# A whole prologue ahead of the first round of scores, in an attention and expert kernel on one Trainium2 core

## The chip, the cores and the metric

The kernel runs on one core of one Trainium2 chip. The metric is the device time of one execution in microseconds (us). Five engines take part, each with its own list of instructions: PE (TensorE, the matmuls), ACT (ScalarE), DVE (VectorE), POOL (GpSimd) and SP (SyncE, which here only issues DMAs). They meet through semaphores: an instruction adds to one when it is done, and another engine waits until it has reached a value.

## The reference, cut to what matters

2048 tokens of 128 features go through an attention layer with 16 heads of 8 features, then through a layer of eight experts of which each token takes two, plus one expert shared by all. The change touches the attention alone:

```python
q = _l2norm(split_heads(x_norm @ Wq))
k = _l2norm(split_heads(x_norm @ Wk))
v = split_heads(x @ Wv)
align = jnp.einsum('bhtd,bhsd->bhts', q, k)
resonance = jax.nn.sigmoid((align - THRESH) * SHARP)
gate_q = jnp.einsum('bhtd,d->bht', q, gq)
gate_k = jnp.einsum('bhsd,d->bhs', k, gk)
modulation = resonance * gate_q[..., :, None] * gate_k[..., None, :]
collapse = jnp.einsum('bhts,bhsd->bhtd', modulation, v)
```

Every query meets every key, so there are 16 x 2048 x 2048 sigmoids.

## The kernel before, in words

**Blocks and rounds.** The queries are cut into four blocks (`NB`) of 512 tokens (`TB`). For each block there are 64 rounds (`ROUNDS`): four sets of four heads, and for each set 16 slices of 128 keys. One round is: PE multiplies the keys of the slice with the queries of four heads (`scores`, L847, matmuls at L862) into two pairs of PSUM banks, ACT takes a sigmoid over each pair (`sigmoids`, L743, the instruction at L746, 128 x 1024 numbers each) and writes them into one half of `res`, and PE multiplies them with the values (`values`, L866, at L876), which add up in the bank `AV` over 16 rounds. PE issues the scores of a round ahead of the value products of the round before. After each 16 rounds DVE multiplies `AV` with the gate of the queries (`collapse`, L1250). In blocks 1 to 3, and in a last stretch without rounds, the work of the experts is laid between the rounds; block 0 has only the preparation of the expert weights on DVE beside it, from round 17 on.

**The prologue.** Before rounds can run, queries and keys have to be made, for four groups of 512 tokens, in six steps on several engines. *tokens*: DVE norms the tokens (L1179), PE transposes them (`turn_hidden`, L800, at L807) and ACT copies them out (L685). *project*: PE multiplies with the weights in four parts (`project_qkv`, L810, L822 to L824), and ACT evicts each (L694); PE goes two parts ahead at most. *square*: ACT squares (L698), DVE sums the squares (L1209), takes an inverse root in some ten small steps and scales the heads (`unit`, L1204, L1215), and makes the gated values (L1221). *high*: ACT makes the high half of queries and keys (L703), DVE the low half (`low_parts`, L1226, L1230), and POOL repeats both (L611, four instructions a group). *turn*: PE transposes queries and keys in four parts (`turn_qk`, L826, L842), and they are copied out, by ACT (`turn`, L706, L713) or, for the last group, by DVE (L1248); each copy adds one to `qk_copied`. Ahead of these last copies DVE makes the weights of the gate (`gate_weights`, L1190, L1192 to L1202).

**Banks.** The prologue uses the banks `GB`, `UB` and `OB`; `UB` and `OB` together are `UO`. A step waits where another still reads its bank: the transposes of the tokens of group 2, for instance, wait for all copies of the turn of group 0, and those of group 3 for the turn of group 1. The rounds use the four banks of `S` as two pairs, and `UO` as a third pair once the prologue has done with it.

**The order.** The list `PROLOGUE` (L89 to L92) sets the order in which PE and ACT issue the steps. ("rounds", n) in it stands for the next n rounds of block 0, on both engines; rounds 0 to 7 stand there, after which the loop over rounds goes on from round 8. DVE and POOL have orders of their own (L1239 to L1248 and L606 to L612), in which rounds do not occur. `WIDE_FROM` (L94) is the round from which the third pair is used: `score_pair` (L97) gives the pair of a half round, `scores_before` (L102) the number of sigmoids after which that pair is free, and in round `WIDE_FROM` PE waits at L859 for all sixteen copies:

```python
if (i, k, j) == (0, WIDE_FROM, 0):

    pe.wait_ge(qk_copied, 4 * NB)
```

Of the kernel before, what the change touches and what calls it, by code (L numbers as in the profile page):

```python
# [86 lines left out]


PROLOGUE = [("tokens", 0), ("project", 0), ("square", 0), ("tokens", 1), ("project", 1), ("high", 0),  # L89
            ("square", 1), ("turn", 0), ("tokens", 2), ("rounds", 1), ("high", 1), ("project", 2),  # L90
            ("square", 2), ("turn", 1), ("tokens", 3), ("rounds", 1), ("high", 2), ("project", 3), ("rounds", 1),
            ("square", 3), ("turn", 2), ("rounds", 2), ("high", 3), ("rounds", 3), ("turn", 3)]  # L92

WIDE_FROM = 9  # L94


def score_pair(n):  # L97

    return (n - 2 * WIDE_FROM) % 3 if n >= 2 * WIDE_FROM else n % 2


def scores_before(n):  # L102

    return max([m + 1 for m in range(max(n - 40, 0), n) if score_pair(m) == score_pair(n)], default=0)
# [16 lines left out]
def build(nc, x, wqkv, vecs, consts, ident16, wo, router, gu, down, out):  # L121
    ctx = ExitStack()
    with ctx:
# [330 lines left out]
        def wait(eng, s, value):  # L454

            if not isinstance(value, int) or value > 0:
                eng.wait_ge(s, value)
# [337 lines left out]
        def _(pe):  # L795
# [51 lines left out]
            def scores(i, k):  # L847
# [5 lines left out]
                for j in range(G):  # L853
                    if j % 2 == 0:

                        wait(pe, sig_done, scores_before(2 * (i * ROUNDS + k) + j // 2))
                        if (i, k, j) == (0, WIDE_FROM, 0):

# [793 lines left out]
```

## Time and profile before

| what | value |
|---|---|
| median of three runs | 727.62 us (724.76 to 728.91) |
| the profiled execution | 728.29 us |
| its span, first to last instruction | 726.5 us |
| mean granted TensorE clock | 0.94 |
| PE busy | 617.6 us (85%) |
| ACT busy | 565.6 us (78%) |
| DVE busy | 419.7 us (58%) |
| POOL busy | 163.4 us (22%) |
| chain that ended last | PE 70%, DVE 13%, issue 5%, ACT 3%, DMA 3%, POOL 2% |
| costliest line of that chain | PE AV L876, 36% |
| sigmoids of `S` and of `UO`, L746 | 348 of mean 1063 ns and 164 of mean 1065 ns |

The profile is of one execution. Times in it count from the start of the span. A row of the timeline gives the start, the time that is covered, the engine, the line of the kernel, the operation, the tile written and the tiles read, and how many instructions were merged; brackets hold the idle time of the engine ahead of it and what ended it. The granted clock is the share of the full 2.4 GHz that TensorE was given; 0.50 is the lower level of 1.2 GHz.

### The profile page before, as it was taken

The page shows a single profiled execution, that of the slowest core. Times are in us where ns is not written, and L with a number is a line of the kernel's source. Part 1 is how long each engine was busy: PE and PEld are TensorE (multiplying, and loading weights), DVE is VectorE, ACT ScalarE, POOL GpSimd, SP SyncE. Part 2 cuts the span into 40 slices and gives each one's busy share as a digit, 9 for nine tenths or more (in the row PEclk, how much of TensorE's full clock was granted, in tenths as well). Part 3 has the DMA queues.
Part 4 walks back from the last instruction along what each step waited for, and adds up shares of the span by engine and source line. Part 5 has one row for each costly group of instructions (what it writes and reads, how often), then busy time and mean ns, then how long its engine had stood idle before and what let it go on. Part 6 is the DMA issues. An engine that isn't in the chain of part 4 may idle for free.

```text
span 726.5 us, 15317 instructions
## 1 busy us (share of the span) xinstructions
PE 617.6 (85%) x5928; PEld 259.6 (36%) x5928; DVE 419.7 (58%) x1105; ACT 565.6 (78%) x663; POOL 163.4 (22%) x149
## 2 busy tenths in 40 slices
PE   3577999999999999999999999989999993475840
PEld 2453211112222344432334444323344441465840
DVE  6775184930552545538635865475458546665975
ACT  1578799999999999989899999888989991033510
POOL 1122000000032122200525212024441210245732
PEclk9999999999999999999999999999999997577975
DMA  8600001630034344410534445105434440293721
GB/s 325 230 30 30 30 9 19 259 111 1 9 107 139 112 132 145 136 51 2 176 116 143 146 130 141 33 22 173 138 113 136 142 131 1 71 333 135 229 79 51
DMA packets 47639, 82.02 MB, mean 113 GB/s; under 512 B 5456, under 2 KB 25168, under 8 KB 47568
## 3 DMA queue, kind: packets, MB, share of 16 engines
q1 hardware_dynamic: 45088, 76.31, 32.8%
q0 software_dynamic: 2048, 4.20, 2.1%
q8 instruction: 47, 0.77, 0.4%
q10 hardware_dynamic: 432, 0.54, 0.3%
q14 instruction: 24, 0.20, 0.1%
HBM read 64.59 MB, written 16.45 MB: 112 GB/s over the span
## 4 chain that ended last, share of the span: by engine, by line
PE 70%; DVE 13%; issue 5%; ACT 3%; DMA 3%; POOL 2%; SPq 1%; POOLq 0%; DVEq 0%
PE AV L876 36%; PE GB L950 14%; PE S L862 7%; PE UO L862 3%; PE GB L897 2%; ACT res L746 1%; DVE work L1381 1%; DVE gate_q L1540 1%; DVE coll L1257 1%; DVE work L1374 1%; PE GB L945 1%; POOL xs_dram L624 1%; DMA gu_ring<-gu_dram 1%; PE UO L842 1%; DVE work L1516 1%
## 5 line engine op out<-in xcount | busy, mean ns | idle before, releaser
L746 ACT ACTIVATE res<-S 128x1024 f32<-128x1024 f32 x348 | 348.8, 1063 | 22.8 <-PE S L862 11.2
L876 PE MATMUL AV<-res,vg 128*8 128x512 f32 x2048 | 305.2, 599 | 1.9 <-DVE coll L1257 1.8
L746 ACT ACTIVATE res<-UO 128x1024 f32<-128x1024 f32 x164 | 174.7, 1065 | 8.5 <-PE S L862 7.2
L650 POOL TENSOR_TENSOR work<-work 128x512 f32<-128x512 f32 x64 | 82.5, 1289 | 290.7 <-DVE work L1381 286.6
L862 PE MATMUL S<-qT,kT 32*128 32x512 f16 x696 | 104.3, 388 | 2.3 <-ACT res L746 2.1
L950 PE MATMUL GB<-xT,gu_ring 128*128 128x128 f16 x1128 | 81.7, 224 | 12.9 <-DVE place L1356 6.0
L721 ACT ACTIVATE work<-work,scl 128x512 f32<-128x512 f32 x64 | 46.7, 730 | 43.5 <-DVE work L1374 43.5
L1374 DVE TENSOR_SCALAR work<-GB,scl 128x512 f32<-128x512 f32 x56 | 45.3, 810 | 59.9 <-PE GB L950 59.3
L862 PEld LDWEIGHTS S<-qT,kT 32*128 32x128 f16 x696 | 25.7, 91 | 145.7 <-ACT res L746 93.5
L950 PEld LDWEIGHTS GB<-xT,gu_ring 128*128 128x128 f16 x1128 | 65.4, 100 | 34.0 <-issue 17.6
L624 POOL DMA_INDIRECT xs_dram<-xrow,slot x32 | 31.7, 990 | 185.4 <-DVE slot L1361 177.1
L862 PE MATMUL UO<-qT,kT 32*128 32x512 f16 x328 | 63.6, 384 | 0.0
L876 PEld LDWEIGHTS AV<-res,vg 128*8 128x8 f32 x2048 | 36.6, 87 | 72.1 <-ACT res L746 29.4
L1393 DVE TENSOR_TENSOR hid_lo<-work,hid_hi 128x512 f16<-128x512 f32 x64 | 49.2, 768 | 5.9 <-ACT hid_hi L736 4.4
L1381 DVE SCALAR_TENSOR_TENSOR work<-work,scl,GB 128x512 f32<-128x512 f32 x48 | 35.8, 746 | 27.6 <-PE GB L950 26.8
L1540 DVE TENSOR_SCALAR gate_q<-GB 128x512 f32<-128x512 f32 x16 | 11.0, 690 | 51.9 <-PE GB L887 51.9
L862 PEld LDWEIGHTS UO<-qT,kT 32*128 32x128 f16 x328 | 15.4, 90 | 67.3 <-ACT res L746 45.7
L950 PE MATMUL GB<-dn_ring,hid_hi 128*128 128x128 f16 x336 | 34.1, 224 | 6.0 <-DVE work L1374 2.6
L1401 DVE COPY xT<-GB 128x256 f16<-128x256 f16 x45 | 12.8, 291 | 38.1 <-PE GB L945 37.9
L1257 DVE TENSOR_TENSOR coll<-AV,gate_q 128x512 f32<-128x512 f32 x16 | 11.0, 689 | 36.1 <-PE AV L876 36.1
L950 PE MATMUL GB<-dn_ring,hid_lo 128*128 128x128 f16 x168 | 31.4, 224 | 0.0
L950 PEld LDWEIGHTS GB<-dn_ring,hid_hi 128*128 128x128 f16 x336 | 24.8, 100 | 16.5 <-issue 7.7
(252 smaller groups left out, 681.0 us busy)
## 6 DMA issues: line engine op xcount, KB each, us to landing
gu_ring<-gu_dram SPq DMA_DIRECT2D x54, 512.0 KB, 3.5
dn_ring<-dn_dram SPq DMA_DIRECT2D x56, 256.0 KB, 2.9
work<-in_gu SPq DMA_DIRECT2D x8, 512.0 KB, 10.5
gu_dram<-gu_ring SPq DMA_DIRECT2D x8, 512.0 KB, 2.7
ys_dram<-work SPq DMA_DIRECT2D x60, 64.0 KB, 2.7
work<-in_down SPq DMA_DIRECT2D x8, 256.0 KB, 10.9
dn_dram<-dn_ring SPq DMA_DIRECT2D x8, 256.0 KB, 2.9
kT<-gu_dram SPq DMA_DIRECT2D x4, 512.0 KB, 7.4
```

Source lines behind the costliest of these rows:

```text
L624: nc.gpsimd.indirect_dma_start(xs_dram, bass.IndirectOffsetOnAxis(ap=slot[:, i % 2, n:n + 1], axis=0), xrow[:, n % SUB, :], None).then_inc ...
L650: nc.gpsimd.tensor_tensor(hid[u % 2], prod[u % 2], sg[u % 2], ALU.mult).then_inc(hid_ready, 1)
L721: nc.scalar.activation(sg[c % 2], gate_c[c % 2], ACT.Sigmoid, scale=scale(S_SIG)).then_inc(sg_ready, 1)
L746: nc.scalar.activation(res[:, k % 2, 2 * half:2 * half + 2, :].rearrange("p h t -> p (h t)"), score_banks(i, k, half).rearrange("p h t -> ...
L862: mm = nc.tensor.matmul(banks[:, j % 2, :], kT[r, g, s * P:(s + 1) * P], qT[r, g, :], start=True, stop=True)
L876: mm = nc.tensor.matmul(AV[32 * j:32 * j + HD, :], vg[:, s, G * g + j, :], res[:, k % 2, j, :], start=s == 0, stop=s == ST - 1)
L950: mm = nc.tensor.matmul(bank, w, v, start=first and n == 0, stop=last and n == 2)
L1257: v.tensor_tensor(coll[:, g, :], AV[:], gate_q[:], ALU.mult).then_inc(coll_ready, 1)
L1374: v.tensor_scalar(gate_c[u % 2], gate_bank(i, u), scale(S_HI), scale(S_LO), ALU.min, ALU.max).then_inc(gate_clipped, 1)
L1381: v.scalar_tensor_tensor(out=prod[u % 2], in0=gate_c[u % 2], scalar=scale(S_PROD), in1=up_bank(i, u), op0=ALU.mult, op1=ALU.mult).then_inc ...
L1393: v.tensor_tensor(hid_lo[:, n % LAG], hid[u % 2], hid_hi[:, n % LAG], ALU.subtract).then_inc(hid_split, 1)
L1540: v.tensor_scalar(gate_q[:], GB[:], 1.0 / QK_SCALE, None, ALU.mult).then_inc(gateb_copied, 1)
```

## The change

The entries of the eight rounds are taken out of `PROLOGUE`, so that all steps of all four groups stand ahead of round 0, and `WIDE_FROM` becomes 0: the third bank pair is in use from round 0, and PE's wait for sixteen copies stands ahead of round 0 instead of round 9. What the rounds compute, and the order of the other steps, stays.

```diff
-            ("square", 1), ("turn", 0), ("tokens", 2), ("rounds", 1), ("high", 1), ("project", 2),
-            ("square", 2), ("turn", 1), ("tokens", 3), ("rounds", 1), ("high", 2), ("project", 3), ("rounds", 1),
-            ("square", 3), ("turn", 2), ("rounds", 2), ("high", 3), ("rounds", 3), ("turn", 3)]
-
-WIDE_FROM = 9
+            ("square", 1), ("turn", 0), ("tokens", 2), ("high", 1), ("project", 2),
+            ("square", 2), ("turn", 1), ("tokens", 3), ("high", 2), ("project", 3),
+            ("square", 3), ("turn", 2), ("high", 3), ("turn", 3)]
+
+WIDE_FROM = 0
```

## Rows read from the trace of the kernel before

**Rows 1.** Windows: length, busy time of each engine, granted clock, DMA share, GB/s.

```profile
82.50:92.50 10.00, 10.00 (x68) 1.64 (x64) 0.00 (x0) 10.00 (x13) 0.00 (x0) 1.00 0.01 2
...
36.30:79.20 42.90, 34.21 (x252) 17.58 (x252) 27.81 (x62) 32.86 (x44) 9.90 (x12) 0.88 0.08 32
```

**Rows 2.** The chain that ended last: start, duration, what; two pieces.

```profile
97.10 1.51 PE AV L876 x8
...
120.94 1.50 PE AV L876 x8
```

**Rows 3.** Timeline of ACT, prologue to round 10.

```profile
20.32 0.50 ACT L694 ACTIVATE pwork<-UO 128x400 f32<-128x400 f32 x1 [0.64 <-PE UO L824]
...
27.31 0.50 ACT L694 ACTIVATE coll<-UO 128x400 f32<-128x400 f32 x1 [0.64 <-PE UO L824]
...
43.59 0.50 ACT L694 ACTIVATE pwork<-UO 128x400 f32<-128x400 f32 x1 [0.64 <-PE UO L824]
...
49.97 0.60 ACT L685 ACTIVATE pwork<-UO 128x512 f32<-128x512 f32 x1 [1.13 <-PE UO L807]
...
64.20 3.93 ACT L746 ACTIVATE res<-S 128x1024 f32<-128x1024 f32 x4
68.03 1.15 ACT L703 ACTIVATE pwork<-coll 128x512 f16<-128x512 f32 x2
...
78.78 3.77 ACT L746 ACTIVATE res<-S 128x1024 f32<-128x1024 f32 x4 [4.05 <-PE S L862]
82.49 1.02 ACT L746 ACTIVATE res<-UO 128x1024 f32<-128x1024 f32 x1
```

**Rows 4.** Timeline of PE, prologue to round 8.

```profile
12.71 1.27 PE L822 MATMUL GB<-w_qkv,lnb_all 128*128 128x272 f32 x2 [0.69 <-ACT pwork L685]
...
22.45 0.72 PE L822 MATMUL GB<-w_qkv,lnb_all 128*128 128x272 f32 x2 [1.73 <-ACT pwork L685]
...
31.53 1.47 PE L842 MATMUL UO<-id,pwork 128*128 128x128 f16 x16 [4.25 <-POOL pwork L611]
33.35 1.92 PE L842 MATMUL UO<-id,pwork 128*128 128x128 f16 x16 [0.35 <-ACT qT L713]
...
37.75 0.73 PE L822 MATMUL GB<-w_qkv,lnb_all 128*128 128x272 f32 x2 [0.36 <-ACT pwork L685]
...
48.94 0.99 PE L807 MATMUL UO<-const_sb,tok 128*128 128x128 f32 x4 [1.18 <-issue]
...
52.23 0.83 PE L822 MATMUL GB<-w_qkv,lnb_all 128*128 128x272 f32 x2
...
63.72 1.90 PE L876 MATMUL AV<-res,vg 128*8 128x512 f32 x8
...
78.35 0.40 PE L862 MATMUL S<-qT,kT 32*128 32x512 f16 x4
```

**Rows 5.** Timeline of DVE, group 3 of the prologue.

```profile
60.50 1.22 DVE L1209 TENSOR_REDUCE ssq<-pwork 128x128 f32<-128x1024 f32 x1 [5.79 <-ACT pwork L698]
...
65.09 1.23 DVE L1215 TENSOR_TENSOR coll<-coll,rn_t 128x1024 f32<-128x1024 f32 x1
...
66.74 0.69 DVE L1221 TENSOR_TENSOR vg<-coll,gk_s 128x512 f32<-128x512 f32 x1
68.69 1.71 DVE L1230 TENSOR_TENSOR pwork<-coll,pwork 128x512 f16<-128x512 f32 x2 [1.25 <-ACT pwork L703]
...
72.69 0.28 DVE L1202 TENSOR_SCALAR gm_b<-const_sb,gq_parts 128x128 bf16<-128x128 f32 x1
76.37 1.29 DVE L1248 COPY y_tok<-UO 128x1024 f16<-128x1024 f16 x2 [3.40 <-PE UO L842]
77.86 1.29 DVE L1248 COPY kT<-UO 128x1024 f16<-128x1024 f16 x2 [0.19 <-PE UO L842]
```

**Rows 6.** Timeline of POOL, group 3 of the prologue.

```profile
68.74 3.30 POOL L611 TENSOR_SCALAR pwork<-pwork 128x512 f16<-128x512 f16 x4 [12.39 <-ACT pwork L703]
```

**Rows 7.** Window with PE's granted clock (1.00, third figure from the end).

```profile
36.40:38.00 1.60, 1.21 (x9) 0.77 (x10) 1.50 (x4) 0.90 (x2) 0.00 (x0) 1.00 0.05 10
```

## The prediction, made before the changed kernel had run

> **What bounds the kernel now.** I read the page first, for the share of the engines and the chain that ended last: it runs mostly through PE, above all through the value products of the rounds, and the slices of the span show that PE and ACT are not yet full in the prologue. Then come the stretches that the change touches. From 82.5 to 92.5 us both engines are busy all the time [rows 1]. The chain of waits shows what a round costs there: from the value products at 97.10 to those at 120.94 lie 13 rounds, so 23.84 / 13 = 1.83 us a round [rows 2]. ACT sets this: its two sigmoids of a round start some 0.91 us apart and follow each other without a gap. A round that isn't done early therefore costs 1.83 us later, and nothing hides it.
>
> In the prologue it is different. From 36.3 to 79.2 us ACT is busy 32.86 of 42.90 us and DVE 27.81 [rows 1]: neither is full, each waits for the other, for PE or for POOL. The sixteen sigmoids of rounds 0 to 7 stand by the list inside the prologue, the four of rounds 8 and 9 start at 78.78 us, and the first of round 10 starts at 82.49 us [rows 3]. From there on the changed kernel issues the same instructions in the same order with the same three bank pairs (the pair of a half round was already its number modulo 3). So the question is one number: **when does the first sigmoid of round 10 start?** Before: 82.49 us. Afterwards: end of the prologue, plus 0.43 us from the first scores at 78.35 to the first sigmoid at 78.78 [rows 3, 4], plus 10 x 1.83 = 18.33 us. The two are equal if the last copies of the prologue end at 82.49 - 18.33 - 0.43 = 63.7 us; they now end at 77.86 + 1.29 = 79.15 us [rows 5]. The prologue would have to become 15.4 us shorter.
>
> **The change part by part.** It takes eight rounds out of three instruction streams (ACT's sigmoids, PE's scores and value products). No DMA is added or removed. The only wait that moves is the one for all sixteen qk_copied copies: from round 9 to round 0, where PE's whole round loop stands behind it, and through it ACT's sigmoids. On SP the store of the last group's queries becomes due earlier with the copies; the next load into qT waits for round 15's scores anyway, and POOL's queue is passed by nothing. I follow the chain with everything at the full clock first.
>
> *Projection of group 2.* Up to its start at 37.75 us nothing changes [rows 4]. Undisturbed, a projection takes 4.86 us from its first matmul to the start of its last eviction (22.45 to 27.31 [rows 3, 4]), so 42.61 us instead of 43.59 [rows 3], where ACT had round 0's sigmoids ahead of the evictions: 0.98 us gained. The square, the turn of group 1 and the transposes of group 3 follow in the same order, so these start at 48.94 - 0.98 = 47.96 us.
>
> *Projection of group 3.* Before, PE did round 1's scores and value products between those transposes and the projection at 52.23 us [rows 4]. Without them it waits only for ACT's copy of their bank, which began 1.03 us after them and took 0.60 [rows 3], so until 49.59 us: start at 49.62, last eviction at 54.48, its square at about 55.0. The square had also stood behind round 2's sigmoids; DVE's reduction of it comes at 56.1 us instead of 60.50 [rows 5], 4.4 us gained.
>
> *DVE's chain of group 3.* From that reduction DVE works without a gap: heads scaled after 65.09 + 1.23 - 60.50 = 5.82 us, values after 66.74 + 0.69 - 60.50 = 6.93 us [rows 5]. This is work, not waiting, and keeps its length: 61.9 and 63.0 us. The high parts on ACT, which stood behind four sigmoids (64.20 to 68.03 [rows 3]), start at 61.95, so the low parts on DVE start at 63.0 instead of 68.69: 5.7 us gained. From the low parts to the end of the gate weights are 72.69 + 0.28 - 68.69 = 4.28 us: 67.3 us.
>
> *Turn of group 3.* POOL's repeats started 0.71 us after ACT's high parts and take 3.30 us [rows 3, 6]; the third of four is through at about 61.95 + 0.71 + 2.5 = 65.2 us, and PE's first transposes (16 in at most 1.92 us at half clock [rows 4]) by 67.1. Before, DVE waited 3.40 us here for a PE that was busy with rounds 5 to 7. That wait goes; **what is late next is DVE itself**, with the 2.65 us of gate weights that it does ahead of the copies and that the wait had covered. So the copies run from 67.3, and their 2.78 us (76.37 to 79.15 [rows 5]) end at 70.1 us: 9.1 us gained of the 15.4 needed. First sigmoid 70.57, round 10 at 88.90, against 82.49: **6.4 us lost**, at the full clock.
>
> *Clock.* Three places may run at half of it. Projection 3: the transposes of 48.94 ran at half clock (0.99 us [rows 4]) and PE stays as idle ahead of them. A projection that began cold took 7.61 us (12.71 to 20.32 [rows 3, 4]) against 4.86, so the price lies between 0 and 2.75 us. I take 1.4: before, the half clock covers the work from 48.94 until shortly after 52.23, where the first pair of matmuls took 0.83 us; if it ends at the same time again, 2.8 us of the projection that now begins at 49.62 run at half speed, and half of that is lost. Turn 3: sixteen cold transposes take 1.92 us [rows 4], at most half of which is the clock: 0 to 0.9, I take 0.4, since PE is nearly idle from 60 us on. First rounds: a cold set of value products takes 1.90 us [rows 4], with 0.4 of scores 0.47 more than a round; for three rounds 0 to 1.4. I take 0.4, because with three pairs PE starts a round ahead and round 0 has no products before it. That the third pair spares ACT its short gaps in rounds 0 to 8 is in the sum already, as each is priced at 1.83.
>
> On the clock two rules of the Trainium skill can be weighed. After 4.25 us of idling PE did two sets of sixteen transposes, the second in 1.92 us at half clock, and nothing else [rows 4]; from 36.4 to 38.0 us the granted clock is 1.00 [rows 7]. The page "TensorE: Matmul & The Clock Gate" of the Trainium skill says, in "Part 1: The HAM clock gate", that the throttled state is the default and that activity releases it; this speaks against the change, which takes scores and value products from between PE's pauses, and by that rule alone the clock terms would be at their upper ends, a loss of 11.5 us in all. The same page adds, in "Part 4: PE-mode transpose", that transpose mode does not count as busy in the same way; by that, turn 3 and the first rounds would be cold throughout, about 1.5 us more than my sum. The trace differs there: the clock rose on transposes alone.
>
> **Sum:** 6.4 + 1.4 + 0.4 + 0.4 = 8.6 us. The profiled execution took 728.29 us (span 726.5), 0.67 above the median of 727.62; from it the sum gives 736.9, and from the median, which is what a comparison sees, **736.2 us**.
>
> **Rivals.** *The waits fall further, and it is not slower.* Place: DVE's waits in the prologue. Price: all that DVE does not work from 36.3 to 79.2 is 42.90 - 27.81 = 15.1 us [rows 1]; were all of it to go, the copies would end at 64.1 and the kernel lose 0.4 us, 728.0. It decides from an end at 63.7 us. For it: every one of these waits is for ACT or PE, whom the change relieves. Against: DVE's reductions need squares of projections that need the bank which the preceding turn frees, and those steps stay. Halfway there, with half of the clock terms, it would lose 3.4 + 1.1 = 4.5: about 732.
>
> *PE cold throughout.* Both projections and all else at half clock: 6.4 + 2 x 2.75 + 0.9 + 1.4 = 14.2 us: 741.8. For it: fewer matmuls between the pauses, as the first clock rule above has it. Against: the clock was full from 36.4 on after transposes alone [rows 7].
>
> *The loss is absorbed later.* A slack in blocks 0 to 3 would take it up, about 727.6. Against: the stretch of [rows 2] is rounds and nothing else, and everything after round 10 is released by rounds, but for the first loads, which SP and ACT issue at the start and wait for nothing.
>
> That the change does something other than it says can be excluded from the code: half rounds 0, 1, 2 get the three pairs, and all users of the two borrowed banks are done when the wait is over.
>
> **How the numbers follow.** Forecast (6.4 to 11.5 us lost) 0.78; waits that fall further, about 4.5 lost, 0.08; down to no loss at all, 0.04; cold throughout 0.06; absorbed 0.04. The range takes in the forecast's bounds and half of the lighter case, less and plus the spread of the runs shown (724.76 to 728.91): 731.5 to 740.0. What such a measurement can tell from no change is about 0.5%, 3.6 us. Slower by more than that has the forecast, the cold case and part of the lighter one: 0.90; same 0.08; faster 0.02.
>
> **What the profile would show.** Right: no sigmoid before about 72 us; projection 3 starting near 49.6; DVE's last copies starting straight after the gate weights, ending at 70 to 73; the first sigmoid of round 10 near 91; after it the same intervals as before. Wrong: copies that end before 66 us, or after 75; a gap between DVE's gate weights and the copies; rounds 0 to 9 that take other than 18 to 19 us; a block 1 whose start is not shifted by the same amount.

## The result, and the profile of the changed kernel

The changed kernel took 741.48 us (median of four runs, 739.86 to 741.79) against 726.19 us before (the three runs of the table and a fourth of 724.05): a ratio of 1.0204, 95% interval 1.0162 to 1.0246, so about 15 us slower. A second set of five runs, taken later, gave 1.0176 (1.0155 to 1.0197), some 13 us. The direction was forecast, the size was not: 736.2 us had been said, and the range ended at 740.0.

The profiled execution has a span of 739.8 us, 13.3 more than before. ACT's timeline answers to [rows 3]; the row at 76.36 is the first sigmoids, and the last row, twenty half rounds on, is the first of round 10:

```profile
42.25 0.50 ACT L694 ACTIVATE pwork<-UO 128x400 f32<-128x400 f32 x1 [1.68 <-PE UO L824]
43.91 0.50 ACT L694 ACTIVATE pwork<-GB 128x400 f32<-128x400 f32 x1 [1.16 <-PE GB L824]
45.05 0.50 ACT L694 ACTIVATE pwork<-UO 128x400 f32<-128x400 f32 x1 [0.64 <-PE UO L824]
...
59.29 0.50 ACT L694 ACTIVATE coll<-UO 128x400 f32<-128x400 f32 x1 [0.64 <-PE UO L824]
...
66.76 1.15 ACT L703 ACTIVATE pwork<-coll 128x512 f16<-128x512 f32 x2 [2.23 <-DVE coll L1215]
76.36 1.94 ACT L746 ACTIVATE res<-S 128x1024 f32<-128x1024 f32 x2 [8.45 <-PE S L862]
...
80.82 1.02 ACT L746 ACTIVATE res<-S 128x1024 f32<-128x1024 f32 x1 [0.68 <-PE UO L862]
...
95.29 1.22 ACT L746 ACTIVATE res<-UO 128x1024 f32<-128x1024 f32 x1
```

Round 10 begins at 95.29 us instead of 82.49: 12.8 of the 13.3 us are lost by then, and the remaining half microsecond is spread over the rest. So the question of the prediction was the right one, and only its answer was off. The bracket of the first sigmoid shows where ACT's time went: it stands 8.45 us ahead of it with nothing to do. Before, its longest wait between 31 and 82 us was 4.05.

DVE's timeline, for [rows 5], and PE's, for [rows 4], show two different things:

```profile
60.92 1.22 DVE L1209 TENSOR_REDUCE ssq<-pwork 128x128 f32<-128x1024 f32 x1 [5.28 <-ACT pwork L698]
...
67.77 2.11 DVE L1230 TENSOR_TENSOR pwork<-coll,pwork 128x512 f16<-128x512 f32 x2
...
69.97 0.38 DVE L1194 TENSOR_TENSOR gq_parts<-vec_sb,gq 128x1 f32<-128x1 f32 x1
...
71.96 0.28 DVE L1202 TENSOR_SCALAR gm_b<-const_sb,gq_parts 128x128 bf16<-128x128 f32 x1
72.15 1.28 DVE L1248 COPY y_tok<-UO 128x1024 f16<-128x1024 f16 x2
74.03 0.69 DVE L1248 COPY kT<-UO 128x1024 f16<-128x1024 f16 x1 [0.59 <-PE UO L842]
74.88 0.69 DVE L1248 COPY kT<-UO 128x1024 f16<-128x1024 f16 x1 [0.16 <-PE UO L842]
```

```profile
30.29 1.86 PE L842 MATMUL UO<-id,pwork 128*128 128x128 f16 x16 [4.25 <-POOL pwork L611]
32.50 1.93 PE L842 MATMUL UO<-id,pwork 128*128 128x128 f16 x16 [0.35 <-ACT qT L713]
35.59 1.09 PE L807 MATMUL UO<-const_sb,tok 128*128 128x128 f32 x4 [1.16 <-issue]
37.36 1.27 PE L822 MATMUL GB<-w_qkv,lnb_all 128*128 128x272 f32 x2 [0.69 <-ACT pwork L685]
...
50.40 1.09 PE L807 MATMUL UO<-const_sb,tok 128*128 128x128 f32 x4 [1.17 <-issue]
52.17 1.27 PE L822 MATMUL GB<-w_qkv,lnb_all 128*128 128x272 f32 x2 [0.69 <-ACT pwork L685]
```

On DVE the forecast order holds: the copies follow the gate weights without a wait (72.15 right behind 71.96), where before there was one of 3.40 us. On PE the clock is the news. Both projections begin with a pair of matmuls of 1.27 us, the length that [rows 4] show for the cold one at 12.71; from the first matmul to the start of the last eviction they take 45.05 - 37.36 = 7.69 and 59.29 - 52.17 = 7.12 us, where the full clock needs 4.86. The window from 31 to 79 us, of the changed kernel and then of the one before, puts a number on it (the clock is the third figure from the end):

```profile
31.00:79.00 48.00, 30.88 (x193) 22.97 (x193) 32.00 (x73) 24.48 (x33) 10.25 (x12) 0.68 0.11 44
```

```profile
31.00:79.00 48.00, 37.41 (x280) 20.36 (x284) 32.66 (x75) 36.50 (x47) 10.86 (x14) 0.86 0.10 38
```

### The profile page after: what moved, and what is told of

It is laid out like the page before. It is cut to its first block, busy times and chain, and to the rows that moved or that the text cites. A ratio compares the mean times of both kernels' runs of the same rounds, so it can differ in the third digit from the quotient of the medians.

```text
span 739.8 us, 15318 instructions
## 1 busy us (share of the span) xinstructions
PE 624.5 (84%) x5928; PEld 264.8 (36%) x5928; DVE 419.7 (57%) x1105; ACT 565.9 (76%) x663; POOL 164.2 (22%) x149
## 4 chain that ended last, share of the span: by engine, by line
PE 73%; DVE 16%; issue 5%; POOL 2%; ACT 2%; DMA 2%; POOLq 0%; DVEq 0%; ACTq 0%
PE AV L876 36%; PE GB L950 15%; PE S L862 7%; PE UO L862 3%; PE GB L897 2%; DVE work L1374 2%; DVE work L1381 2%; DVE gate_q L1540 1%; DVE coll L1257 1%; PE GB L822 1%; PE GB L945 1%; POOL res L638 1%; DVE work L1516 1%; PE UO L950 1%; PE UO L842 1%
## 5 line engine op out<-in xcount | busy, mean ns | idle before, releaser
L746 ACT ACTIVATE res<-S 128x1024 f32<-128x1024 f32 x342 | 344.9, 1073 | 27.8 <-PE S L862 15.7
L746 ACT ACTIVATE res<-UO 128x1024 f32<-128x1024 f32 x170 | 182.4, 1073 | 8.5 <-PE S L862 7.2
L862 PE MATMUL S<-qT,kT 32*128 32x512 f16 x684 | 102.6, 388 | 1.6 <-DVE kT L1248 0.9
L862 PE MATMUL UO<-qT,kT 32*128 32x512 f16 x340 | 66.5, 388 | 0.0
L1401 DVE COPY xT<-GB 128x256 f16<-128x256 f16 x45 | 12.8, 291 | 38.2 <-PE GB L945 37.9
```

The lines of the kernel that those rows point to most:

```text
L746: nc.scalar.activation(res[:, k % 2, 2 * half:2 * half + 2, :].rearrange("p h t -> p (h t)"), score_banks(i, k, half).rearrange("p h t -> ...
L862: mm = nc.tensor.matmul(banks[:, j % 2, :], kT[r, g, s * P:(s + 1) * P], qT[r, g, :], start=True, stop=True)
```

## The experiments

Theory A: the rounds' sigmoids lose their cover, as forecast, and the clock falls further than priced. Rival B: the order of the steps costs all of it, and the half clock only goes along.

**Extra matmuls in PE's pauses.** `filler(n)` puts n matmuls of 272 columns into a score bank that round 0 overwrites; nobody reads them.

```diff
+            def filler(n):
+                for _ in range(n):
+                    nc.tensor.matmul(S[:, 0, 0:2 * D + H], lnb_all[:], w_qkv[:, 0:2 * D + H], start=True, stop=True)
...
+                        if b in (1, 2):
+                            filler(1)
                         pe.wait_ge(qk_copied, b * 4 + n - 1)
...
                     tokens += 1
+                    filler(1 if b > 1 else 0)
...
                     projected += 1
+                    filler(8 if b == 1 else 1 if b > 1 else 0)
...
                     turned += 1
+                    filler((2, 2, 14, 0)[b])
```

> The changed kernel, with extra matmuls of no use on PE wherever it pauses in the prologue (272 columns into a score bank that nobody reads before round 0 overwrites it), so that nothing but the granted clock should change. Theory A, the step that failed is the clock term: the granted clock is near 1.00 in the prologue, both late projections take about 4.9 us from first matmul to last eviction instead of 7.1 to 7.7, the first sigmoid of round 10 comes 6 to 8 us earlier than at 95.3 us, and the time is 733 to 736 us. Theory B, the half clock only goes along and the order of the steps costs the 15 us: about 741 us, or more where the extra matmuls get in the way.

Measured: 732.55 us (five runs, 731.38 to 733.7), ratio to the kernel before 1.0064 (1.0044 to 1.0083). By the ratios, useless work made the changed kernel 8 to 10 us faster. Its window, then rows of ACT and of PE:

```profile
31.00:79.00 48.00, 41.13 (x289) 25.87 (x288) 32.16 (x74) 30.61 (x40) 10.39 (x12) 0.96 0.11 45
```

```profile
41.49 0.50 ACT L694 ACTIVATE pwork<-UO 128x400 f32<-128x400 f32 x1 [0.64 <-PE UO L824]
...
53.13 0.50 ACT L694 ACTIVATE coll<-UO 128x400 f32<-128x400 f32 x1 [0.64 <-PE UO L824]
...
69.34 1.94 ACT L746 ACTIVATE res<-S 128x1024 f32<-128x1024 f32 x2 [7.59 <-PE S L869]
...
73.79 1.02 ACT L746 ACTIVATE res<-S 128x1024 f32<-128x1024 f32 x1 [0.68 <-PE UO L869]
...
88.26 1.22 ACT L746 ACTIVATE res<-UO 128x1024 f32<-128x1024 f32 x1
```

```profile
70.73 2.48 PE L883 MATMUL AV<-res,vg 128*8 128x512 f32 x8
73.14 0.61 PE L869 MATMUL S<-qT,kT 32*128 32x512 f16 x2
```

The granted clock is 0.96, the projections take 5.12 and 4.98 us, and round 10 begins at 88.26, against 95.29 without the extra matmuls: 7.0 us of the 12.8 go with the clock. About 0.5 of the 7.0 is won ahead of the transposes of group 2's tokens (35.06 us against 35.59), where none of the removed rounds had stood. One place stayed cold: the first value products and the scores behind them, where the granted clock is 0.50 from 72 to 74 us. The spans of the two profiles differ by 10.1 us; the 3.1 that lie behind round 10 can't be put down to the edit, because the same instructions stand there in every kernel of this document and took 641.4 to 646.2 us in the twelve profiles.

Theory B is out. What is left is near the part of the prediction worked out at the full clock, which had round 10 at 88.90.

**The third bank pair alone.** The changed kernel with its pairs as before:

```diff
-WIDE_FROM = 0
+WIDE_FROM = 9
```

> The changed kernel with the third bank pair from round 9 only, as before: the first part of the change alone. Theory A (three pairs from round 0 are worth little, but keep ACT fed while PE is cold): 0.5 to 2 us slower than the changed kernel, 742 to 743.5 us. Theory C (the early wait or the early third pair costs something): equal to the changed kernel or faster, 741.5 us or less.

Measured: 739.25 us, ratio 1.0158 (1.013 to 1.0186), so not slower than the changed kernel. My expectation fell. ACT's rows say why:

```profile
75.36 3.77 ACT L746 ACTIVATE res<-S 128x1024 f32<-128x1024 f32 x4 [6.94 <-PE S L862]
80.00 15.07 ACT L746 ACTIVATE res<-S 128x1024 f32<-128x1024 f32 x16 [0.86 <-PE S L862]
94.96 1.02 ACT L746 ACTIVATE res<-UO 128x1024 f32<-128x1024 f32 x1
```

Rounds 0 to 9 take 94.96 - 75.36 = 19.6 us on two pairs, 95.29 - 76.36 = 18.9 on three. But on two pairs round 0 needn't wait for DVE's last copies, which end here at 75.84: it starts 0.5 us ahead of them, while in the changed kernel it starts 0.8 us behind them (76.36 against 75.57). The third pair gains 0.7 us and its wait takes 1.3, and the runs show no gain from the two together. What lies in the order of the prologue is practically the whole loss.

**Three of the eight rounds.** The kernel before, with rounds 5 to 7 behind the last turn:

```diff
-            ("square", 3), ("turn", 2), ("rounds", 2), ("high", 3), ("rounds", 3), ("turn", 3)]
+            ("square", 3), ("turn", 2), ("rounds", 2), ("high", 3), ("turn", 3)]
-WIDE_FROM = 9
+WIDE_FROM = 6
```

> The kernel before with only rounds 5 to 7 moved behind the last turn, and the third pair from round 6. Theory A: three rounds put off cost 5.5 us, the wait of DVE for PE of 3.4 us goes; the first sigmoid of round 10 moves from 82.5 to about 85.4, with up to 1 us for a colder clock: 729 to 731 us. Theory B' (each of the eight rounds costs its eighth of the 15 us): 732 us. If the rounds were free in either place: 726 us.

Measured: 730.16 us (ten runs), ratio 1.0034 (1.0014 to 1.0054); round 10 begins at 86.12, 3.6 us later than before, as theory A had it with its 1 us for a colder clock (group 2's projection, whose instructions are those of before, took 1.1 us longer here). An equal share of the loss for each round, 3 / 8 of 15 us, would have been 5.6.

**Gate weights behind the copies.** In the changed kernel:

```diff
-            gate_weights()
-
             dve.wait_ge(q_saved, (NB - 1) * 16)
             for n in range(4):
                 dve.wait_ge(qk_tr, (NB - 1) * 4 + n + 1)
                 v.tensor_copy(*turned_bank(NB - 1, n)).then_inc(qk_copied, 1)
+            gate_weights()
```

> The changed kernel with DVE's gate weights (2.65 us) behind the last copies of the prologue instead of ahead of them. Theory A: they are on the path, but right behind them PE's cold transposes would be late next (first half done at about 71.4 us against copies that start at 72.15), so 0.7 us is gained, about 740.8 us. If DVE alone were late: 2.65 us, 738.8 us. If the gate weights were not on the path: 741.5 us.

Measured: 737.38 us, ratio 1.0123 (1.009 to 1.0156), more than expected. But round 0 gained 76.36 - 73.70 = 2.66 us in the profile, of which 66.76 - 64.90 = 1.86 are there already when ACT makes the high parts of group 3, ahead of anything that the edit touches. That leaves 0.8 us for it, as expected. The rest is a warmer group 2: its projection took 6.54 us here instead of 7.69. The transposes ahead of it ran at the full clock (0.63 us) and its first pair nearly so, but then it fell to half clock all the same:

```profile
37.70 0.95 PE L822 MATMUL GB<-w_qkv,lnb_all 128*128 128x272 f32 x2 [0.69 <-ACT pwork L685]
...
39.78 1.11 PE L822 MATMUL UO<-w_qkv,lnb_all 128*128 128x272 f32 x2
```

DVE's rows, here with a wait of 1.74 us for PE's cold transposes, confirm what is late next:

```profile
69.75 1.48 DVE L1246 COPY y_tok<-UO 128x1024 f16<-128x1024 f16 x2 [1.74 <-PE UO L842]
71.64 1.49 DVE L1246 COPY kT<-UO 128x1024 f16<-128x1024 f16 x2 [0.41 <-PE UO L842]
...
73.22 0.16 DVE L1194 TENSOR_TENSOR gq_parts<-vec_sb,gq 128x1 f32<-128x1 f32 x1
```

**The same two again**, to see what was chance.

> The changed kernel itself once more, on the same chip and beside the same runs of the kernel before as the three kernels below. If the granted clock of the prologue falls differently in each execution, times between 737 and 743 us; the middle is what the others are held against.

> The changed kernel with the gate weights behind the last copies, once more, with more executions: the profile of the first try gave them 0.8 us and the rest of its gain to a warmer clock in projections that the edit can't touch. If that was chance: 0.5 to 1.5 us faster than the changed kernel, ratio to the kernel before about 1.016. If the edit is worth more than the profile shows: about 1.012 again.

Measured: the changed kernel 739.47 us (738.94 to 743.11), ratio 1.0176; with the late gate weights 737.33 (735.79 to 741.7), ratio 1.0155 (1.0114 to 1.0196). The profiles of this pair show the same division as the first: round 10 begins 2.47 us earlier (92.62 against 95.09), of which 1.71 are there at the high parts of group 3, so 0.8 is left for the edit. The gap in the runs, 0.2 to 0.3%, lies within the intervals. So most of the 4 us of the first try was chance, in its profile a warmer clock ahead of the edit.

**PE's part of the removed rounds, without ACT's.** A list entry that only PE heeds stands at the five old places; for each round it issues four score matmuls and, from round 1 on, two matmuls of 272 columns in place of the value products. The outputs are overwritten.

```diff
+                elif what == "blind":
+                    for k in range(blind, blind + b):
+                        for j in range(G):
+                            r = slice(32 * j, 32 * j + 32)
+                            nc.tensor.matmul(S[:, j, :], kT[r, 0, k * P:(k + 1) * P], qT[r, 0, :], start=True, stop=True)
+                        if k > 0:
+                            for _ in (0, 1):
+                                nc.tensor.matmul(S[:, 0, 0:2 * D + H], lnb_all[:], w_qkv[:, 0:2 * D + H], start=True, stop=True)
```

> The changed kernel, with PE alone doing at the eight old places what it did there before: the four score matmuls of a round into banks that are overwritten later, and two matmuls of 272 columns in place of its value products; ACT does nothing there. Theory A (it is the PE work of the removed rounds that had kept the clock up): granted clock from 31 to 79 us near the 0.86 of before instead of 0.68, first sigmoid of round 10 some 4 to 6 us earlier than 95.3, 734 to 737 us. Theory B (the clock of the profiled executions fell as it did by chance, and this little work changes nothing): within 2 us of the changed kernel.

Measured: 735.95 us, ratio 1.0122 (1.0102 to 1.0141) beside the changed kernel's 1.0176: about 4 us faster, for doing more. Its window and PE's two projections:

```profile
31.00:79.00 48.00, 39.39 (x267) 25.47 (x265) 31.89 (x73) 27.04 (x36) 10.26 (x12) 0.82 0.11 45
```

```profile
37.34 1.27 PE L822 MATMUL GB<-w_qkv,lnb_all 128*128 128x272 f32 x2
...
39.73 0.62 PE L822 MATMUL UO<-w_qkv,lnb_all 128*128 128x272 f32 x2
...
51.23 1.11 PE L822 MATMUL GB<-w_qkv,lnb_all 128*128 128x272 f32 x2
...
53.42 0.62 PE L822 MATMUL UO<-w_qkv,lnb_all 128*128 128x272 f32 x2
```

Both projections still begin cold, but have the full clock at their second part; in the changed kernel only at the third or fourth. Round 10 begins at 92.73 us, 2.6 earlier than in the changed kernel; 4 to 6 had been expected, so only part of the clock's loss comes back. All profiles without extra work on PE agree with this one: group 3's projection took 6.54 to 7.20 us in the five of the changed order, 4.96 to 5.30 in the three that have a round there, and 5.81 here. So the removed rounds had, besides their own work, kept PE's clock up: theory A.

**All that lay bare taken off.** The changed order with the extra matmuls of the first experiment, the late gate weights, and the third pair from round 3, so that round 0 needn't wait for the last copies:

```diff
-WIDE_FROM = 0
+WIDE_FROM = 3
```

> The changed order with all that was found to bare it taken off: PE kept busy in its pauses, the gate weights behind the copies, and the third pair from round 3 only, so that round 0 does not wait for the last copies. If what is left is the sixteen sigmoids that no longer run beside the prologue: the first sigmoid of round 10 near 86.5 us against 82.5 before, ratio 1.003 to 1.005. If the whole prologue can be as fast as the mixed one once the clock is up: ratio 1.000 or less.

Measured: 731.45 us (twelve runs), ratio 1.0063 (1.0041 to 1.0085; 1.003 to 1.005 had been expected), with a granted clock of 1.00 from 31 to 79 us. Rows of ACT, then of PE:

```profile
67.90 7.49 ACT L746 ACTIVATE res<-S 128x1024 f32<-128x1024 f32 x8 [5.71 <-PE S L869]
...
86.19 1.17 ACT L746 ACTIVATE res<-UO 128x1024 f32<-128x1024 f32 x1
```

```profile
70.21 1.04 PE L883 MATMUL AV<-res,vg 128*8 128x512 f32 x8
```

Round 10 begins at 86.19 us, 3.7 later than before (86.5 had been expected); the 2 us that the profile gains on the first experiment don't show in the ratio. From the first sigmoid to round 10 ACT now works without a gap, 18.29 us. So what the clock does not explain fits the ACT time that no longer overlaps with the prologue.

**The other direction.** The kernel before, with its last turn cut in two around round 7, and the gate weights behind the copies; then the same with extra matmuls in three pauses (eight ahead of the turn of group 0, two behind it, two behind that of group 1).

```diff
-            ("square", 3), ("turn", 2), ("rounds", 2), ("high", 3), ("rounds", 3), ("turn", 3)]
+            ("square", 3), ("turn", 2), ("rounds", 2), ("high", 3), ("rounds", 2), ("turn_first", 3), ("rounds", 1), ("turn_last", 3)]
...
+                elif what in ("turn_first", "turn_last"):
+                    turn_qk(b, projected, tokens, (0, 1) if what == "turn_first" else (2, 3))
```

> The other direction: the kernel before with its rounds left in the prologue, the last turn cut in two halves around round 7 so that ACT has round 7's sigmoids while DVE copies, and the gate weights behind the copies. If ACT's only long wait (4.05 us ahead of round 8) is what is left to gain: ACT waits some 1 to 2 us there, 2 to 3 us faster than the kernel before, ratio 0.996 to 0.997. If PE's order only moves the wait elsewhere: no difference.

> The same, with extra matmuls of no use in PE's three longest pauses of the prologue (before and after the turn of group 0, after the turn of group 1), to hold the clock up. By the clock theory 2 to 4 us faster than the split kernel, ratio to the kernel before 0.991 to 0.994; if the kernel before is warm enough in its prologue, equal to the split kernel.

Measured: 724.51 us, ratio 0.9973 (0.9958 to 0.9989), and 723.82 us, 0.9963 (0.9943 to 0.9983). Both are faster than both kernels. ACT's timeline of the first:

```profile
72.92 1.94 ACT L746 ACTIVATE res<-S 128x1024 f32<-128x1024 f32 x2 [0.95 <-PE S L862]
75.22 3.77 ACT L746 ACTIVATE res<-S 128x1024 f32<-128x1024 f32 x4 [0.36 <-PE S L862]
78.94 1.02 ACT L746 ACTIVATE res<-UO 128x1024 f32<-128x1024 f32 x1
```

Of the wait of 4.05 us 0.95 + 0.36 are left, as expected, and round 10 begins at 78.94. The extra matmuls, worth 8 to 10 us in the changed kernel, can't be told from nothing in the runs here; in the profile round 10 begins 1.4 us earlier with them (77.53). The split kernel's granted clock from 31 to 79 us was 0.87 without them and 0.93 with them, so there was less to win back. Whether sigmoids beside a cold projection would also hide it was not tried.

## Why the prediction was right about the sign and wrong about the size

The step that failed is the clock part of the sum: 2.2 us were put in, of them nothing for group 2's projection, and 95.29 - 88.90 = 6.4 came. Against the sum at the full clock the profile is 2.4 us late at the last eviction of group 2 (45.05 for 42.61), 4.8 at that of group 3 (59.29 for 54.48), 5.5 at the end of the copies (75.57 for 70.1) and 6.4 at round 10.

- **What bounds it, and the break-even at 63.7 us**: right. The copies end at 74.88 + 0.69 = 75.57 us, and the loss is fixed by round 10.
- **Projection of group 2**: here the sum failed first. It had the full clock, and no clock term at all, since "nothing changes" ahead of it and [rows 7] show 1.00. Ahead of the transposes of group 2's tokens nothing did change, but the clock of one execution isn't that of the next. These transposes, which took 0.63 us in the profile of before, took 1.09 in that of the experiment with three rounds moved and in that of the split turn, whose instructions up to there are those of before. The projection itself cost 7.69 - 4.86 = 2.8 us more. That much was chance only in part: behind the transposes something did change, because round 0's scores had stood between them and the projection (36.99 us), and in the changed order it took 6.54 to 7.86 us in all five profiles without extra work on PE, 6.54 also where the transposes were warm. So a term of 1.7 us or more was missing in any case.
- **Projection of group 3**: its start hung on that. Its clock term, 1.4 in a bound of 0 to 2.75, measured 7.12 - 4.86 = 2.3.
- **DVE's chain, the gate weights, "late next is DVE itself"**: right; from the reduction to the copies 72.15 - 60.92 = 11.23 us, forecast 67.3 - 56.1 = 11.2.
- **Turn of group 3**: 2.78 us taken for the copies plus 0.4 for the clock; measured 75.57 - 72.15 = 3.42. Nearly right.
- **First rounds**: the term of 0.4 was nearly right in size (rounds 0 to 9 take 18.93 us instead of 18.33), and the runs bear out its cause. The gap of 0.68 us ahead of the fifth sigmoid is there in the first experiment too, but there the first value products ran at half clock again (2.48 us). On two pairs the gap is 0.86 us with cold value products (0.50 granted from 78 to 80 us), and with warm ones, in the experiment with all taken off (1.04 us), there is none.
- **The clock terms together**: 2.2 us were taken, and 6.4 came; the first experiment, which removes all but those of the first rounds, gained 7.0 at round 10. That is the mis-sized term. The rival "PE cold throughout", 741.8 us at a chance of 0.06, came nearest, but its clock terms add up to 7.8, and PE was not cold throughout: the last parts of both projections had the full clock (0.62 us a pair). That 741.48 lies so near its 741.8 is partly luck, as the profiles differ by 13.3 us and the medians by 15.3.
- **The weighing of the two rules**: the Trainium skill's page "TensorE: Matmul & The Clock Gate" says in "Part 1: The HAM clock gate" that activity releases the throttle. By that rule the loss had been put at 11.5 us. The experiment with PE's part of the rounds agrees, with 0.82 granted instead of 0.68. The same page of the Trainium skill says in "Part 4: PE-mode transpose" that transpose mode doesn't count as busy in the same way; against that I had set one row of before. In the changed kernel two sets of transposes from 30.29 to 34.43 us left those at 35.59 cold (1.09 us), as that rule has it; of the nine profiles without extra matmuls ahead of that place six look like this and three like before. Why it differs between executions was not settled.
- **The full-clock loss of 6.4 us**: right to within 0.6 us at round 10 (88.90 forecast, 88.26 measured), partly because two things cancel: the extra matmuls let group 2's projection begin 1.4 us earlier than at 37.75, and the cold first rounds take 0.6 back. In runs the warm kernel is 0.64% slower than before, some 4.7 us.
- **The signs**: one sign of being wrong came, copies that end after 75 us. Projection 3 began at 52.17 instead of near 49.6, and round 10 at 95.29 instead of near 91. The copies straight behind the gate weights, the length of rounds 0 to 9 and the equal shift of all that follows came as said.

## What to carry to other kernels

Work that is laid between the steps of a prologue can pay twice, as it did here: its own engine's time overlaps, and with it PE had a granted clock of 0.86 in the prologue, without it 0.68. Before a term is priced from one profile's granted clock, its instruction should be looked at in a second execution; if its length differs there, both lengths belong in the range. And where moving work away bares a chain, look for what had been hidden behind that work: here DVE's gate weights, which had run in a wait for PE, and then stood on the chain.

## What the runs showed of the hardware that had not been expected

Matmuls that nobody reads made a kernel 8 to 10 us faster in runs, and 7.0 of it stand at round 10 of the profile, where the granted clock of the prologue went from 0.68 to 0.96. PE ran one projection of the same instructions in 6.54 to 7.86 us from one profile to the next. And a subtraction of single columns on DVE (L1194) took 0.38 us while POOL was at its repeats, and 0.16 once it was done, in the experiment with the late gate weights; the copies of single columns next to it (L1195) took 0.16 in both. The gate weights as a whole went from 2.44 to 2.03 us with it. That POOL is the cause was not tried.
